# Where the matmul operands begin in SBUF: moving ones at 224, stationary ones at 32 modulo 256 bytes

## The reference

```
xn  = layernorm(x)                              # no affine
# s: linear attention over xn, 16 heads of 64, then a feed-forward of 1024
q, k, v = xn@Wq+bq, xn@Wk+bk, xn@Wv+bv
Q, K = elu(q)+1, elu(k)+1
KV = einsum('bshd,bshm->bhdm', K, v)
Z  = 1/(einsum('bshd,bhd->bsh', Q, K.sum(1)) + 1e-6)
o  = einsum('bshd,bhdm,bsh->bshm', Q, KV, Z)
x1 = LN(xn + o@Wo + bo; g1, be1)
s  = LN(x1 + gelu(x1@W1+b1)@W2 + b2; g2, be2)
# g: gate, up and down projections (704 wide), operands quantised to FP4 by blocks of 16
h  = silu(fp4(xn)@fp4(w_gate).T) * (fp4(xn)@fp4(w_up).T)
g  = silu(fp4(h)@fp4(w_down).T)
out = x + s*g
```

## Time and profile before

| | |
|---|---|
| Median of 3 runs | 1679.24 us (1677.78 to 1679.68) |
| Profiled execution, its own time | 1680.37 us |
| Its span, first to last instruction | 1678.5 us |
| Granted TensorE clock, mean over the span | 0.996 |
| PE busy | 1644.1 us (98%), 11105 matmuls |
| DVE / ACT / POOL busy | 79% / 58% / 46% |
| DMA | 89.36 MB, 15.9% of the engines' time |

### The profile page before, as it was taken

One profiled execution on the slowest core, in us unless ns is written; L12 is line 12 of the kernel. 1 busy time (PEld: TensorE's weight loads), 2 busy tenths in 40 slices (PEclk: granted clock), 3 DMA queues, 4 the chain that ended last, 5 costly groups with the idle time before them and its releaser, 6 DMA issues.

```text
span 1678.5 us, 30547 instructions
## 1 busy us (share of the span) xinstructions
PE 1644.1 (98%) x11105; PEld 1469.2 (88%) x11105; DVE 1322.8 (79%) x2587; ACT 967.5 (58%) x1754; POOL 778.4 (46%) x718
## 2 busy tenths in 40 slices
PE   7999999999999999999999999999999999999997
PEld 6878888888889898989999998989898999999897
DVE  6685664555879797979889797979797988979797
ACT  6665656655464646565655556464646565555644
POOL 4564543434134444444453534444444446353446
PEclk9999999999999999999999999999999999999999
DMA  7322323422200101021010102010101201010100
GB/s 230 130 77 89 106 66 116 121 91 91 93 1 1 51 1 51 19 86 52 1 51 2 51 2 104 2 51 2 51 19 34 77 29 51 1 51 2 51 1 26
DMA packets 69986, 89.36 MB, mean 53 GB/s; under 512 B 8383, under 2 KB 54603, under 8 KB 68814
## 3 DMA queue, kind: packets, MB, share of 16 engines
q1 hardware_dynamic: 69838, 87.42, 15.9%
HBM read 53.30 MB, written 34.10 MB: 52 GB/s over the span
## 4 chain that ended last, share of the span: by engine, by line
PE 54%; DVE 12%; issue 4%; ACT 1%; POOL 1%; DVEq 0%; ACTq 0%
PE QH L81 7%; PE QH L83 6%; PE QH L82 6%; PE AC L81 6%; PE AC L83 6%; PE AC L82 6%; PE GU L81 4%; PE GU L83 4%; PE GU L82 4%; PE TT L816 3%; DVE hb L1760 1%; DVE bslna L1840 1%; DVE hb L1758 1%; PE QH L714 1%; DVE AC L1831 1%
## 5 line engine op out<-in xcount | busy, mean ns | idle before, releaser
L1212 ACT ACTIVATE rh<-QH 128x512 fp32r<-128x512 f32 x256 | 147.1, 595 | 84.2 <-DVE QH L1918 80.1
L81 PE MATMUL GU<-wgh,xqh 128*128 128x352 f32 x512 | 171.2, 334 | 8.9 <-DVE hb L1760 8.8
L2416 POOL TENSOR_TENSOR hb<-hb,rs_h 128x704 f32<-128x704 f32 x64 | 89.1, 1392 | 170.0 <-DVE rs_h L1767 170.0
L82 PE MATMUL GU<-wgl,xqh 128*128 128x352 f32 x512 | 165.7, 324 | 0.0
L83 PE MATMUL GU<-wgh,xql 128*128 128x352 f32 x512 | 165.6, 323 | 0.0
L1933 DVE TENSOR_TENSOR rl<-QH,rh 128x512 fp32r<-128x512 f32 x128 | 85.7, 689 | 95.1 <-ACT rh L1212 74.7
L81 PE MATMUL AC<-Mh,rh 128*128 128x256 f32 x512 | 145.7, 285 | 0.0
L81 PE MATMUL AC<-w2h,rh 128*128 128x256 f32 x512 | 144.2, 282 | 0.0
L82 PE MATMUL AC<-Ml,rh 128*128 128x256 f32 x512 | 142.8, 279 | 0.0
L83 PE MATMUL AC<-Mh,rl 128*128 128x256 f32 x512 | 142.7, 279 | 0.0
L82 PE MATMUL AC<-w2l,rh 128*128 128x256 f32 x512 | 142.4, 278 | 0.0
(11 more groups left out here) (241 smaller groups left out, 5711.1 us busy)
## 6 DMA issues: line engine op xcount, KB each, us to landing
xa<-in_L_attn_src SPq DMA_DIRECT2D x16, 512.0 KB, 4.2
xt_scratch<-xth SPq DMA_DIRECT2D x32, 256.0 KB, 2.6
xt_scratch<-xtl SPq DMA_DIRECT2D x32, 256.0 KB, 3.0
xb<-in_L_attn_src SPq DMA_DIRECT2D x16, 512.0 KB, 4.2
xnTh<-xt_scratch SPq DMA_DIRECT2D x32, 256.0 KB, 4.7
xnTl<-xt_scratch SPq DMA_DIRECT2D x32, 256.0 KB, 5.4
out<-x SPq DMA_DIRECT2D x15, 512.0 KB, 6.6
m_scratch<-mh SPq DMA_DIRECT2D x16, 256.0 KB, 2.4
```

Of the source, the lines that this page charges most:

```text
L81: e.matmul(outp, lh, rh, start=start, stop=False, skip_group_check=check)
L82: e.matmul(outp, lh, rl, start=False, stop=False, skip_group_check=check)
L1212: e.activation(RH[j % 4][:], src, ACT.Copy).then_inc(S[sem], 1)
L2416: e.tensor_tensor(hb, hb, spread(rs_h[i % 2][:], 44), ALU.mult).then_inc(S["hin"], 1)
```

## The change

Seven unused buffers of 32 to 192 bytes are put between the others, of three old ones two go and one shrinks, and nothing else is touched. No instruction, no order, no wait and no size of an operand changes.

```
-        sb("before_weights", [128, 24])
+        sb("gap_wq", [128, 40])
         wqh, wql = sb("wqh", [128, 2, 1024], F32R), sb("wql", [128, 2, 1024], F32R)
         w1h, w1l = sb("w1h", [128, 2, 1024], F32R), sb("w1l", [128, 2, 1024], F32R)
+        sb("gap_w2", [128, 48])
         w2h, w2l = sb("w2h", [128, 8, D], F32R), sb("w2l", [128, 8, D], F32R)
...
-        sb("after_weights", [128, 8])
...
+        sb("gap_x", [128, 16])
...
+        sb("gap_xt", [128, 16], F32, A1)
         xth = [sb(f"xth{i}", [128, 2, D], F32R, A1) for i in range(2)]
...
+        sb("gap_sel", [128, 16])
         sel, sel16, sg = sb("sel", [128, 8, 128], F32R), sb("sel16", [128, 16]), sb("sg", [128, 2])
...
+        sb("gap_xq", [128, 8])
         xqh, xql = sb("xqh", [128, 2, D], F32R), sb("xql", [128, 2, D], F32R)
...
-        sb("main_rest", [128, 682])
+        sb("main_rest", [128, 576])
...
+        sb("gap_rh", [128, 16])
         RH = [sb(f"rh{i}", [128, 512], F32R) for i in range(4)]
```

## The result

| | before | after |
|---|---|---|
| Median | 1679.24 us (1677.78 to 1679.68) | 1685.38 us (1684.74 to 1686.65) |
| Ratio | | 1.0034, 95% interval 1.0023 to 1.0045 |
| Span of the profiled execution | 1678.5 us | 1683.6 us |
| Granted TensorE clock | 0.996 | 0.998 |

The changed kernel is slower by 0.34%. The forecast was 1670.7 us with a range of 1658 to 1680, so the time lies above the range, and it moved the other way. What came is the mechanism of the third rival: 512 columns are worse at 224 and 32.

The account below looks back on a forecast made before the run. PE, busy 98% of the span, was taken as the bound through its matmul steps. Second-phase terms 4.4 + 1.3 + 3.1 + 0.4 + 1.5 = 10.7 us, 0.8 of it 8.6, gave a median of 1670.7 us, range 1658 to 1680.

Parts of the forecast that it names:

- third rival: 512-column products: steps get longer at 224 and 32, first phase costs 8.8 us; time 1690 us, chance 0.09.
- Term 7: First phase, K and K by x to 224 and 32: 0; bounds 2.8 us gained, 4.3 us lost.
- Term 4: W1 from 32 and 224 to 224 and 32: 0.4 us gained; bounds 2.2 lost and 2.2 gained.
- Term 3: q projection from 192 and 224 to 224 and 32: 3.1 us gained; bounds 0.8 and 5.1.
- Term 1: M products from 96 and 32 to 224 and 32: 4.4 us gained; bounds 0 and 6.6.
- Term 2: W2, place unchanged: long steps behind q go if q leaves a cleaner state, 1.3 us gained; bounds 0 and 3.
- Term 6: Down projection, place unchanged: 0; at most 2 us if its entries from gate and up become clean.
- Term 5: Gate and up, stationary side from 160 to 32: 1.5 us gained, nothing if only distance counts; ceiling 6.1 us.
- The share on the path: Second phase: 0.8 of the terms' sum shortens the span, the rest turns into longer waits for DVE; 8.6 us.
- first rival: All matmul runs: operand streams' alignment at entry decides the step, place only by chance; 1677 to 1681 us, chance 0.13.

Follow-up runs that it names:

- e5_k_alone: Kernel before with the K side alone moved from 192 and 192 to 224 and 32 (distance 0 to 192); 1685.04 us, ratio 1.0035.
- e6_q_zero: Kernel before with wqh and wql alone moved from 224 to 192, so q has distance 0; 1679.02 us, ratio 0.9994.
- e3_wide_192: Whole change at 256 and 352 columns, but all 512-column products at 192 and 192; 1677.21 us, ratio 0.9991.
- e1_m_only: Kernel before with M's moving operands Mh and Ml alone moved from 96 to 224; 1679.47 us, ratio 0.9999.
- e9_turn_32: Kernel before with Mh and Ml at 224 and the transposes' operands moved (ident, hb to 32; Q32, ksB, vectors and others along); 1680.67 us, ratio 1.0007.
- e4_same_place: Kernel before with distance 0 everywhere: K side and q at 224, W1, W2 and M at 32, gate, up and down at 96; 1688.78 us, single run.
- e7_low_apart: Kernel before with the K side's low stationary parts (xtl, xnl) alone moved from 192 to 0; 1685.41 us, single run.
- e2_wide_back: Whole change with its 512-column products (K side, spread of Z, q, W1) put back to their old places; 1679.78 us, ratio 1.0002.
- e11_best2: Whole change with the K side put back to 192 and 192 and W1 at its old distance of 64; 1678.23 us, ratio 0.9992.

## Why the prediction was wrong, point by point

- **What bounds the kernel.** Right: PE's steps carry the time. But in the first phase 7.3 us of matmul time became only 5.9 us of span (5.7 in e5_k_alone), 0.8 of it, where I had counted all of it. The 7.3 us price all 1536 matmuls; the 1440 or so whose steps were measured make 6.8 of it, and the rest of that phase took about 1 us less. Why it did is open.
- **The inference that failed** stands in the first part: what lies above the clean step is about as much at 256 columns as at 512, so it belongs to the load and not to the columns. From that I carried 224 and 32, good at 256 columns, over to 512. But the same distance is good at one width and bad at the other: 0 gives 226.7 and 120.0, 192 gives 233.3 and 113.3. The size per matmul is alike; which distance has it isn't.
- **Term 7, K and K by x, taken as 0**: measured +7.3 us of matmul time. The bound of 4.3 us lost took 229.1 for the worst step, a row of the present W1 at another distance, though rows 6 and 10 had 233.0 and 232.0. With 233.0 in its place the bound would have been 6.7 ns a matmul over rows 9, some 10 us, and a high end with this added would have been past 1685.4. The 1.8 ns of its bound on the gain has no row behind it.
- **Term 4, W1, taken as a gain of 0.4**: lost 2.6. **Term 3, q, 3.1**: 0.2 lost; e6_q_zero and e3_wide_192 show that q could gain 2.2 to 2.5, at distance 0.
- **Term 1, M, 4.4**: gained 3.4, but not for the reason given, so that it came near is luck. M alone at its new place gains nothing (e1_m_only); with the operands of the transposes moved too, it gained 2.8 (e9_turn_32).
- **Term 2, W2, 1.3**: gained 0.9, but its runs at the long step didn't go: of 97 runs of nine matmuls or more 32 had 117.7 or 117.8 before and 30 after. **Term 6, down, 0**: lost 1.0. It isn't the gate's new place alone: in e9_turn_32 gate and up hadn't moved, and down had 116.3 all the same, against 115.1.
- **Term 5, gate and up, 1.5**: 0.2 lost. One of the text's two readings gave no gain, but not for the right reason. If the distance counted, the halves would have traded their steps. They didn't: the slices at distance 64 had 160.2 ns and those at 192 had 159.7 before, and after the trade it was 160.2 for those now at 192 and 160.0 for those now at 64. So 160 on both halves doesn't say that the distance counts.
- **The share on the path, 0.8**, wasn't tested by a clear second-phase change; q in e6_q_zero gave 2.2 us of matmul time, 0.6 us of the median and 2.0 us of the second phase in one trace, so the share stays open. The forecast's own high end, 1677, doesn't follow from its terms: half of M and q, nothing from gate and up is 5.4 us, 0.8 of it 4.4, and so 1675. That slip of 2 us is not what failed.
- **The rivals.** The third had the mechanism, the place and the point from which it decides (the first phase's step over 228 ns for more than half). It priced the loss at 8.8 us of matmul time there, and 7.3 was measured; it added 2 us for M and W2, which went the other way, so 1690 and not 1685.4. Its chance was set low although no row spoke against it: no row showed 512 columns at this pair at all. The first rival, luck of entry, had its part too: at 256 columns something other than a run's own place picks between 113.3 and 117.7.
- **The rule in the Trainium skill**, "TensorE: Matmul & The Clock Gate", step-by-step part of "What happens when you issue a matmul", that loading the next stationary operand takes no SBUF read bandwidth from the running matmul. The prediction drew from it that the two operands' places would not matter to one another. That conclusion falls: with the same instructions in the same order, e5_k_alone lost 0.35% by moving the starts of the operands, and e4_same_place put both elsewhere at the old distance and had the old steps. The rule itself isn't settled by this: in e7_low_apart the step that grew most, by 4 to 5 ns, was that of the matmul that holds the displaced part, and the one beside which that part is loaded grew by 1 ns.

## What to carry to other kernels

Where PE bounds a kernel of split float32r products, the distance between the starts of the moving and the stationary operand modulo 256 bytes is worth up to 3% of a matmul at 512 columns (226.7 to 233.3 ns) and up to 6% at 256 (113.3 to 120.0), and costs some bytes of padding. It can lose more than it wins: moving the K side off distance 0 cost 5.4 us of the median (e5_k_alone), and no placement won more than 2.5 us over the kernel before. Measure it for each width: here 0 was best at 512, 192 at 256, and 352 hardly cared. Don't add up prices from different layouts, since a run's step also depends on what else lies where. And never carry a row from one width to another: for a value that no row shows take the worst row at that width as its bound, not the nearest.

Two traces are compared stretch by stretch only after their granted clock has been: with the K side at its old steps, the first phase took 396.3 and 396.6 us in the traces without a stretch at 1.2 GHz in it, 397.7 to 398.5 with one, and 400.0 and 400.1 with one twice as long. With the K side at 224 and 32 it was 404.2 and 404.0, with one.

## What the runs showed of the hardware that was not expected

- On the K side the absolute place made no difference while the distance stayed 0: 228.8 and 228.1 ns at 224 and 224 (a single run), 228.7 and 228.2 at 192 and 192.
- The good distances are isolated. At 512 columns 0 and 64 are short (226.7, 228.9), and 32 between them is 233.
- At 256 columns and a distance of 192 there are two settled steps, 113.3 and 117.8 ns, each kept for runs of up to 36 matmuls. Moving other buffers, operands of the transposes among them, changes which one most runs have (M 117.3 to 115.5 and W2 115.2 to 117.5 with neither moved). Both steps were also seen at a distance of 64.
- In the K side with the low parts displaced, the long step was L83's (233.5 ns), which holds the displaced part, and not L82's (229.7), beside which it is loaded. Which of the reads is slowed stays open.
- 352 columns step 159.8 to 160.8 ns at seven of eight distances, 4 to 5 ns over 352 times the clean rate. No placement tried gave the clean 156 ns for a whole product.
- PE's clock fell to 1.2 GHz at about 48 us in some traces (granted clock 0.51 from 48.0 to 51.4 us before), though PE was busy all the time ahead of it and in it, 3.40 us of 3.40 in each. In e2_wide_back and e11_best2 it kept 2.4 GHz there. Each such stretch made the first phase some 1.8 us longer.
